# A graph layer whose gathers are issued by GpSimd: the low edge part in two halves, and one wait of VectorE removed

## The chip, the cores and the metric
The kernel runs on one core of a Trainium2 chip. Its time is the device time of one execution in microseconds (us). Three runs of the kernel before gave 1126.44, 1127.38 and 1129.05 us; the median is 1127.38 us.

The core's engines are named as the profile names them: PE (TensorE, matrix products; PEld is its weight load), DVE (VectorE), ACT (ScalarE), POOL (GpSimd) and SP (SyncE, which issues transfers here). Each runs its own list of instructions in order, and they wait for one another by semaphores.

## The reference
There are 6250 nodes with 256 features and 106250 edges, sorted by their target node `dst`. All is in float32.

```
h   = relu(layernorm(x))                          # 6250 x 256
eq  = h @ Wq + bq ;  ek = h @ Wk + bk             # per node
e   = edge_attr_256 @ We + be                     # per edge, 106250 x 256
m   = relu(eq[dst] + ek[src] + e)                 # per edge
ft  = segment_sum(m, dst, 6250)                   # per node
out = x + ft @ Wr + br
```

`src` is random, so the rows `ek[src]` have to be gathered.

## The kernel before
**Start.** The nodes' `ek` and the first rows of `eq` are computed and stored in tables in HBM (`k_table`, `q_table`). This takes some 70 us. The rest of `eq` is computed beside the edge loop.

**Edge loop.** The edges are taken in 208 groups of 512 (the last one has 3 tiles of 128 edges instead of 4). Four groups make a body; in `visit(it, u)`, `n` is the number of the group and `slot` is `n % 4`. Numbers are split in two parts for the products: a high part rounded to the format that PE multiplies, and a low part with what is left, so that each product is made of three (high x high, high x low, low x high). For one group:

- SP loads the edge features, already turned (`edge`, 4 buffers, `load_edge`, L416), the targets' positions (`rel_row`) and a window of 48 rows of `eq` (`q_win`).
- POOL writes the four gathers of the rows of `ek` (`gather`, L701; the instruction is at L714), one for each tile of 128 edges, into `k_rows`. Four buffers; it may go on when group n - 4 has been added (`s_pre`). Each gather counts up `s_wrote` when its descriptors are written, and `s_rows` when its rows have landed. Group 0 has no gather from the table: it is computed at the start from rows of `x` that four gathers brought (L654), which count up `s_wrote` too.
- ACT makes the high edge part (`edge_hi`, L809) two groups ahead, and DVE the low edge part (`edge_low`, L1155, `edge_lo = edge - edge_hi`, L1159), also two groups ahead, in one instruction over 128 x 1024.
- PE makes the product (`edge_product`, L1441), with a last matmul that picks the rows of `q_win`. It is made one group ahead. It waits for the low message part of group n - 2 (`s_mlo`), whose `p_edge` buffer it takes over.
- DVE adds the gathered rows to the product (`add_rows`, L1172, the addition at L1184), ACT makes the high message part (`m_hi`, L866), DVE the low one (`message_low`, L1188, at L1193).
- DVE makes a matrix of ones and zeros (`send`, L1167) by which PE sums the messages into a window of 48 nodes (`window_sum`); the sum is turned by PE and DVE adds it to `ft` (L1208). Once per body a block of 128 nodes goes through `Wr` to the output.

**Order on VectorE.** It is written out by hand. For group u of a body: add_rows(u), send(u), the ft addition of group u - 3, edge_low(u + 2), message_low(u), and then, in some groups of a body, one or two small instructions (L1226, L1215, L1232, L1238, L1243). PE's order for the same step is edge_product(u + 1), window_sum(u - 1), turn of u - 2.

**The wait that is removed.** Before the addition for group n, DVE waits for `s_wrote >= 4 (n + 2)`, that is until all gathers of group n + 1 have been written (LEAD is 2 and TILES is 4), besides the waits for the product of group n (`s_prod`) and for its own rows having landed (`s_rows`). In the last body this wait is left out for the last two groups.

**Why PE has no wait for the low edge part.** On DVE, edge_low(n) stands before message_low(n - 2), and PE waits for the latter; so only the first two groups wait for `s_elo`.

Of the kernel before, what the change touches and what calls it, by code (L numbers as in the profile page):

```python
# [26 lines left out]
HALVES = D // LANES  # L27
BLOCKS = 52
ROWS = BLOCKS * LANES
TILES = 4  # L30
GROUP = TILES * LANES
GROUPS = -(-EDGES // GROUP)
UNROLL = 4
# [31 lines left out]
LEAD = 2  # L65
# [21 lines left out]
def gnn_program(nc, x, dst_groups, dst_lanes, src_lanes, edges, Wq, bq, Wk, bk, We, be, Wr, br, out):  # L87
    F32, F32R = mybir.dt.float32, mybir.dt.float32r
# [14 lines left out]
    with ctx:  # L103
        def sb(name, shape, dt):
            return ctx.enter_context(nc.sbuf_tensor(name, shape, dt))
# [4 lines left out]
        def sem(name):  # L110
            return ctx.enter_context(nc.semaphore(name))
# [58 lines left out]
        edge = sb("edge", [LANES, 4, HALVES, GROUP], F32)  # L170
        edge_hi = sb("edge_hi", [LANES, 2, HALVES, GROUP], F32R)
        edge_lo = sb("edge_lo", [LANES, 2, HALVES, GROUP], F32R)
# [108 lines left out]
        s_wrote = sem("gather_descriptors_written")  # L281
        s_go_act = sem("scalar_may_go_on")
        s_idx = sem("idx_ready")
        s_ehi = sem("edge_hi_ready")
        s_elo = sem("edge_lo_ready")
# [24 lines left out]
        def after(eng, semaphore, n):  # L310


            if isinstance(n, int) and n < 0:
                return
            eng.wait_ge(semaphore, n + 1)
# [17 lines left out]
        def visit(it, u):  # L333

            body, slot = it + u // UNROLL, u % UNROLL
            return body, slot, body * UNROLL + slot, body // BODIES, body % BODIES
# [41 lines left out]
        def _(sp):  # L378
# [37 lines left out]
            def load_edge(it, u):  # L416
                body, slot, n, _, gb = visit(it, u)

                after(sp, s_elo, n - 4)
                g = gb * UNROLL + slot  # L420
                src = edges[g] if isinstance(g, int) else edges[bass.ds(g, 1)].rearrange("a p h e -> (a p) h e")
                sp.dma_start(edge[:, slot], src).then_inc(s_edge[slot], 16)
# [561 lines left out]
        def _(dve):  # L984
# [167 lines left out]
            window_starts()  # L1152
            window_table()

            def edge_low(it, u):  # L1155
                body, slot, n, _, _ = visit(it, u)

                after(dve, s_ehi, n)
                nc.vector.tensor_tensor(edge_lo[:, slot % 2], edge[:, slot], edge_hi[:, slot % 2].bitcast(F32),  # L1159
                                        ALU.subtract).then_inc(s_elo, 1)  # L1160

            def make_send(it, u):
# [9 lines left out]
            def add_rows(it, u, last=False):  # L1172
                body, slot, n, _, _ = visit(it, u)
                tiles = LAST_TILES if last and u == UNROLL - 1 else TILES
                cols = slice(0, tiles * D)

                if not (last and u + LEAD >= UNROLL):
                    dve.wait_ge(s_wrote, TILES * (n + LEAD))
                after(dve, s_prod, n)
                if isinstance(n, int) and n == 0:  # L1180
                    after(dve, s_kcopy, ALL_BLOCKS - 1)
                else:
                    dve.wait_ge(s_rows[slot], 16 * TILES * (body if slot > 0 else body - 1) + 16 * tiles)
                nc.vector.tensor_tensor(p_edge[:, slot % 2, cols], p_edge[:, slot % 2, cols],  # L1184
                                        k_rows[:, slot].rearrange("p t d -> p (t d)")[:, cols], ALU.add)\
                    .then_inc(s_pre, 1)

            def message_low(it, u, tiles=TILES):  # L1188
                _, slot, n, _, _ = visit(it, u)
                cols = slice(0, tiles * D)  # L1190

                after(dve, s_mhi, n)
                nc.vector.scalar_tensor_tensor(m_lo[:, slot % 2, cols], p_edge[:, slot % 2, cols], 0.0,  # L1193
                                               m_hi[:, slot % 2, cols].bitcast(F32), ALU.max, ALU.subtract)\
                    .then_inc(s_mlo, 1)

            def window_of(it, u):
                _, slot, _, ps, gb = visit(it, u)
                w = dve.value_load(win_tab[0:1, bass.ds(gb * UNROLL + slot, 1)], min_val=0, max_val=NODES - WIN)
                return window_start(dve, w, ps)  # L1200
# [19 lines left out]
            def finish(it):  # L1220

                after(dve, s_outp, it)
                dve.wait_ge(s_xo, (it + 1) * 16)
                if not (isinstance(it, int) and it == 0):
                    dve.wait_ge(s_out, it * 16)
                nc.vector.tensor_tensor(result[:, 0, :], p_res, out_x[:, 0, :], ALU.add).then_inc(s_fin, 1)  # L1226
# [24 lines left out]
            def steps(it, first=False, q=False):  # L1251
                for u in range(UNROLL):
                    if not (first and u < 3):
                        w0 = window_of(it, u - 3)
                    if u == 3 and isinstance(it, int) and it <= CLEAR_BODIES:
                        dve.wait_ge(s_cleared, it + 1)
                    if u == 2:
                        after(dve, s_fhi, it)
                    if u == 3:
                        after(dve, s_flo, it)  # L1260
                    add_rows(it, u)
                    make_send(it, u)
                    if not (first and u < 3):
                        add_sum(it, u - 3, w0)
                    edge_low(it, u + 2)
                    message_low(it, u)
                    if u == 0 and isinstance(it, int) and it < CLEAR_BODIES:
                        clear(it + CLEAR_AHEAD)
                    if u == 0 and first:
                        dve.wait_ge(s_unused, 1)  # L1270
                    if u == 3 and first:
                        output_bias_low()
                    if u == 1 and q:
                        next_h_low(it)
                    if u == 3 and q:
                        next_q_low(it)
                    if u == 2:
                        if not first:
                            finish(it - 1)
                        ft_low(it)  # L1280
# [10 lines left out]
            nc.vector.tensor_tensor(rel_idx[:], dst_idx[:], win_f[:].unsqueeze(2).to_broadcast(  # L1291
                [LANES, GROUPS, TILES]), ALU.subtract).then_inc(s_prep, 1)
            for u in range(2):
                edge_low(0, u)
            dve.wait_ge(s_hn0, ALL_PAIRS)
            dve.wait_ge(s_hn1, ALL_PAIRS)
            clear(0, CLEAR_AHEAD)
# [4 lines left out]
            for it in range(1, STATIC_BODIES):  # L1302
                steps(it, q=it < Q_BODIES)
# [11 lines left out]
            def last_steps(it):  # L1315
                for u in range(3):
                    w0 = window_of(it, u - 3)
                    if u == 2:
                        after(dve, s_fhi, it)
                    add_rows(it, u, True)  # L1320
                    make_send(it, u)
                    add_sum(it, u - 3, w0)
                    if u < 2:
                        edge_low(it, u + 2)
                        message_low(it, u)
                finish(it - 1)
                ft_low(it)
                w0 = window_of(it, 0)
                add_rows(it, 3, True)
                after(dve, s_flo, it)  # L1330
                dve.wait_ge(s_fhi, it + 2)
                add_sum(it, 0, w0)
                message_low(it, 2)
                add_sum(it, 1, window_of(it, 1))
                make_send(it, 3)
                message_low(it, 3, LAST_TILES)
                add_sum(it, 2, window_of(it, 2))
                finish(it)
                tail_low(0)
                w0 = window_of(it, 3)  # L1340
                after(dve, s_flo, it + 1)
                add_sum(it, 3, w0)
                for t in range(1, len(TAIL)):
                    tail_low(t)
# [10 lines left out]
        def _(pe):  # L1355
# [85 lines left out]
            def edge_product(it, u, tiles=TILES):  # L1441
                body, slot, n, _, _ = visit(it, u)


                if isinstance(n, int) and n < 2:
                    after(pe, s_elo, n)
                after(pe, s_pick, n)
                pe.wait_ge(s_win[slot], 32 * (body + 1))
                after(pe, s_mlo, n - 2)
                for j in range(tiles):  # L1450
                    target = p_edge[:, slot % 2, j * D:(j + 1) * D]
                    tile = slice(j * LANES, (j + 1) * LANES)
                    split_product(target, lambda h: edge_hi[:, slot % 2, h, tile],
                                  lambda h: edge_lo[:, slot % 2, h, tile], we_hi, we_lo, stop=False)
                    ins = nc.tensor.matmul(target, pick[:, slot % 2, tile], q_win[:, slot, :],  # L1455
                                           start=False, stop=True)
                ins.then_inc(s_prod, 1)
# [145 lines left out]
```

## Time and profile before
| | |
|---|---|
| three runs | 1126.44, 1127.38, 1129.05 us |
| profiled execution | 1127.15 us |
| its span | 1125.3 us |
| granted TensorE clock, mean | 0.998 of full speed |
| PE busy | 1085.7 us (96%) |
| DVE busy | 952.0 us (85%) |
| ACT busy | 855.8 us (76%) |
| POOL busy | 843.3 us (75%) |
| DMA | 308.88 MB, 274 GB/s on average |

The times of instructions come from one profiled execution; its time was 1127.15 us, of which the span of the profile is 1125.3 us. "Busy" is the time in which an engine ran instructions; the issue of DMAs and the handling of semaphores is not in it, except that POOL's gathers count while their descriptors are written. "Idle before" with a name after it says which engine's work or which transfer ended an idle time.

### The profile page before, as it was taken

To read this page: it belongs to the slowest core of one execution; us is meant where nothing else is said; L and a number is where in the kernel's file an instruction comes from. 1 tells how busy PE (TensorE), PEld (TensorE's weight loads), DVE (VectorE), ACT (ScalarE), POOL (GpSimd) and SP (SyncE) were. 2 spreads that over 40 slices of the span, in tenths; PEclk is the share of its full clock that TensorE was granted. 3 is DMA by queue.
4 is the path that set the end of the run, shared out by engine and by line. 5 is a ranking of instruction groups with operands and counts; after the bars stand their busy time and mean duration, and the time that the engine had idled before them with its cause. 6 is when DMAs were issued, how large, how long until landed. Compare 5 with 4: busy or idle time off the path is not lost.

```text
span 1125.3 us, 28375 instructions
## 1 busy us (share of the span) xinstructions
PE 1085.7 (96%) x9170; PEld 1063.5 (95%) x9170; DVE 952.0 (85%) x1425; ACT 855.8 (76%) x1373; POOL 843.3 (75%) x947
## 2 busy tenths in 40 slices
PE   8989999999999999999999999999999999999997
PEld 8989999999999999999999999999999999998997
DVE  7878888888888888888888888888888888887886
ACT  7968877777777777777777778777787777876774
POOL 8877777777777777777777777777777777777773
PEclk9999999999999999999999999999999999999999
DMA  9889999999999999999999899999898998998882
GB/s 299 267 241 304 288 281 275 286 276 288 278 282 285 278 285 278 280 282 276 287 277 280 284 272 288 274 283 285 271 290 274 285 287 273 288 278 268 265 252 86
DMA packets 170744, 308.88 MB, mean 274 GB/s; under 512 B 30568, under 2 KB 116981, under 8 KB 170661
## 3 DMA queue, kind: packets, MB, share of 16 engines
q1 hardware_dynamic: 130212, 198.57, 53.4%
q0 software_dynamic: 39888, 108.97, 35.8%
q14 instruction: 69, 0.56, 0.1%
q10 hardware_dynamic: 560, 0.52, 0.1%
q8 instruction: 15, 0.25, 0.1%
HBM read 280.99 MB, written 26.95 MB: 274 GB/s over the span
## 4 chain that ended last, share of the span: by engine, by line
POOL 72%; issue 24%; PE 1%; DVE 1%; ACT 1%; DMA 1%; POOLq 0%; ACTq 0%; DVEq 0%; SPq 0%
POOL k_rows L714 69%; POOL hn L641 1%; PE p_sum L1360 0%; POOL window_cols L592 0%; DMA src_idx<-in_src_lanes 0%; POOL edge L654 0%; PE p_edge L1360 0%; ACT k_rows L784 0%; ACT hn L757 0%; PE p_sum L1476 0%; DVE stats L1002 0%; PE p_turn L1380 0%; DVE m_lo L1193 0%; DMA k_rows<-k_table,idx 0%; POOL norm L619 0%
## 5 line engine op out<-in xcount | busy, mean ns | idle before, releaser
L714 POOL DMA_INDIRECT k_rows<-k_table,src_idx x796 | 764.1, 960 | 242.8 <-issue 242.8
L1360 PE MATMUL p_edge<-we_hi,edge_hi 128*128 128x256 f32 x1662 | 471.7, 284 | 28.6 <-DVE m_lo L1193 27.3
L1360 PE MATMUL p_edge<-we_hi,edge_lo 128*128 128x256 f32 x1662 | 461.3, 278 | 0.0
L1360 PE MATMUL p_edge<-we_lo,edge_hi 128*128 128x256 f32 x1662 | 460.0, 277 | 0.0
L1184 DVE TENSOR_TENSOR p_edge<-p_edge,k_rows 128x1024 f32<-128x1024 f32 x208 | 256.1, 1231 | 153.5 <-DMA k_rows<-k_table,src_idx 112.8
L866 ACT ACTIVATE m_hi<-p_edge 128x1024 fp32r<-128x1024 f32 x208 | 213.8, 1028 | 204.6 <-DVE p_edge L1184 204.6
L1360 PEld LDWEIGHTS p_edge<-we_hi,edge_hi 128*128 128x128 f32 x1662 | 313.4, 189 | 46.6 <-ACT pick L858 21.4
L1360 PEld LDWEIGHTS p_edge<-we_lo,edge_hi 128*128 128x128 f32 x1662 | 314.3, 189 | 0.0
L1360 PEld LDWEIGHTS p_edge<-we_hi,edge_lo 128*128 128x128 f32 x1662 | 312.1, 188 | 0.0
L1159 DVE TENSOR_TENSOR edge_lo<-edge,edge_hi 128x1024 fp32r<-128x1024 f32 x208 | 253.5, 1219 | 0.0
L1193 DVE SCALAR_TENSOR_TENSOR m_lo<-p_edge,m_hi 128x1024 fp32r<-128x1024 f32 x208 | 253.3, 1218 | 0.0
L1455 PE MATMUL p_edge<-q_win,pick 98*128 98x256 f32 x831 | 233.2, 281 | 0.0
L809 ACT ACTIVATE edge_hi<-edge 128x1024 fp32r<-128x1024 f32 x208 | 217.8, 1048 | 2.3 <-PE p_edge L1455 2.2
L1476 PE MATMUL p_sum<-m_hi,send 128*48 128x256 f32 x831 | 200.7, 278 | 0.6 <-DVE m_lo L1193 0.6
L1476 PE MATMUL p_sum<-m_lo,send 128*48 128x256 f32 x831 | 200.4, 278 | 0.0
L1455 PEld LDWEIGHTS p_edge<-q_win,pick 98*128 98x128 f32 x831 | 156.0, 188 | 0.0
L855 ACT ACTIVATE rel_g<-rel_row,lane_node 96x512 int16<-96x512 int16 x208 | 147.2, 708 | 4.5 <-DMA rel_row<-rel_table 4.5
L858 ACT ACTIVATE pick<-rel_g 96x512 fp32r<-96x512 int16 x208 | 131.6, 633 | 6.6
L873 ACT ACTIVATE sum_rows<-p_sum 48x256 f32<-48x256 f32 x208 | 77.3, 372 | 33.3 <-PE p_sum L1476 29.7
L1476 PEld LDWEIGHTS p_sum<-m_hi,send 128*48 128x48 f32 x831 | 101.2, 122 | 0.9 <-DVE m_lo L1193 0.9
L1476 PEld LDWEIGHTS p_sum<-m_lo,send 128*48 128x48 f32 x831 | 101.0, 121 | 0.0
L1465 PE MATMUL p_turn<-ident,sum_rows 128*128 128x128 f32 x416 | 79.4, 272 | 0.9 <-ACT sum_rows L873 0.9
(159 smaller groups left out, 1111.2 us busy)
## 6 DMA issues: line engine op xcount, KB each, us to landing
edge<-in_edges SPq DMA_DIRECT2D x208, 512.0 KB, 5.2
rel_row<-rel_table SPq DMA_DIRECT2D x208, 96.0 KB
q_win<-q_table SPq DMA_DIRECT2D x416, 48.0 KB
k_rows<-k_table,src_idx POOLq DMA_INDIRECT x796
q_table<-hn SPq DMA_DIRECT2D x46, 256.0 KB
pre<-in_x SPq DMA_DIRECT2D x55, 128.0 KB, 3.7
out_rows<-pre SPq DMA_DIRECT2D x55, 128.0 KB, 1.7
k_table<-k_rows SPq DMA_DIRECT2D x23, 256.0 KB, 3.5
```

Of the source, the lines that this page charges most:

```text
L714: nc.gpsimd.indirect_dma_start(out=k_rows[:, slot, j, :], out_offset=None, in_=k_table, in_offset=bass.IndirectOffsetOnAxis(ap=offsets, ax ...
L809: nc.scalar.activation(edge_hi[:, slot % 2], edge[:, slot], ACT.Copy).then_inc(s_ehi, 1)
L855: nc.scalar.activation(gap[:], rel_row[:, slot, :], ACT.Abs, scale=-1.0, bias=lane_node[:, bass.ds(ps, 1)]).then_inc(s_gap, 1)
L858: nc.scalar.activation(pick[0:2 * WIN, slot % 2, :], gap[:], ACT.Relu, bias=1.0, scale=-1.0)\
L866: nc.scalar.activation(m_hi[:, slot % 2, cols], p_edge[:, slot % 2, cols], ACT.Relu).then_inc(s_mhi, 1)
L1159: nc.vector.tensor_tensor(edge_lo[:, slot % 2], edge[:, slot], edge_hi[:, slot % 2].bitcast(F32), ALU.subtract).then_inc(s_elo, 1)
L1184: nc.vector.tensor_tensor(p_edge[:, slot % 2, cols], p_edge[:, slot % 2, cols], k_rows[:, slot].rearrange("p t d -> p (t d)")[:, cols], AL ...
L1193: nc.vector.scalar_tensor_tensor(m_lo[:, slot % 2, cols], p_edge[:, slot % 2, cols], 0.0, m_hi[:, slot % 2, cols].bitcast(F32), ALU.max, A ...
L1360: ins = nc.tensor.matmul(target, a(h), b[:, h, :], start=(start and h == 0 and n == 0), stop=(stop and h == HALVES - 1 and n == 2))
L1455: ins = nc.tensor.matmul(target, pick[:, slot % 2, tile], q_win[:, slot, :], start=False, stop=True)
L1465: ins = nc.tensor.transpose(p_turn[:, 0, h * LANES:(h + 1) * LANES], sum_rows[:, slot % 2, h * LANES:(h + 1) * LANES], ident[:])
L1476: ins = nc.tensor.matmul(p_sum[0:WIN, 0, 0:D], send[:, slot % 2, j, :], m[:, slot % 2, j * D:(j + 1) * D], start=(j == 0 and m is m_hi), s ...
```

## The change
It has two parts. The low edge part is computed in two instructions of 128 x 512 instead of one of 128 x 1024: the first before the low message part, the second behind it. The semaphore `s_elo` therefore counts two for each group, and those who wait for it are adapted: SP before it loads the next edges into the buffer, and PE, which now waits for the second half before every edge product, since that half no longer stands before message_low. The other part: the wait of DVE for `s_wrote` is taken out of `add_rows`.

```diff
@@ load_edge (SP)
-                after(sp, s_elo, n - 4)
+                after(sp, s_elo, HALVES * (n - 4) + HALVES - 1)
@@ edge_low (VectorE)
-            def edge_low(it, u):
+            def edge_low(it, u, h):
                 body, slot, n, _, _ = visit(it, u)
-                after(dve, s_ehi, n)
-                nc.vector.tensor_tensor(edge_lo[:, slot % 2], edge[:, slot], edge_hi[:, slot % 2].bitcast(F32),
+                if h == 0:
+                    after(dve, s_ehi, n)
+                nc.vector.tensor_tensor(edge_lo[:, slot % 2, h], edge[:, slot, h], edge_hi[:, slot % 2, h].bitcast(F32),
                                         ALU.subtract).then_inc(s_elo, 1)
@@ add_rows (VectorE)
-                if not (last and u + LEAD >= UNROLL):
-                    dve.wait_ge(s_wrote, TILES * (n + LEAD))
                 after(dve, s_prod, n)
@@ steps (VectorE), and the same in last_steps for u < 2
-                    edge_low(it, u + 2)
+                    edge_low(it, u + 2, 0)
                     message_low(it, u)
+                    edge_low(it, u + 2, 1)
@@ before the loop (VectorE)
             for u in range(2):
-                edge_low(0, u)
+                for h in range(HALVES):
+                    edge_low(0, u, h)
@@ edge_product (PE)
-                if isinstance(n, int) and n < 2:
-                    after(pe, s_elo, n)
+                after(pe, s_elo, HALVES * n + HALVES - 1)
                 after(pe, s_pick, n)
```

## Rows read from the trace of the kernel before

**Rows 1.** The page's first parts: span, busy time by engine, chain that ended last.
```profile
span 1125.3 us, 28375 instructions
...
PE 1085.7 (96%) x9170; PEld 1063.5 (95%) x9170; DVE 952.0 (85%) x1425; ACT 855.8 (76%) x1373; POOL 843.3 (75%) x947
...
POOL 72%; issue 24%; PE 1%; DVE 1%; ACT 1%; DMA 1%; POOLq 0%; ACTq 0%; DVEq 0%; SPq 0%
```

**Rows 2.** Waits, whole run: who waited for whom: us in total, times, longest.
```profile
POOL k_rows L714 <- issue: 252.0, 826, 0.6
...
PE p_edge L1360 <- DVE m_lo L1193: 27.3, 59, 1.3
```

**Rows 3.** The gathers' line: duration ns min/median/max, first and last start us.
```profile
L714 POOL DMA_INDIRECT k_rows<-k_table,src_idx x796: 942/946/1966, 64.5 to 1069.8; - x199
```

**Rows 4.** Gathers by stretch: stretch, us, POOL busy (x instructions), clock, DMA.
```profile
64.40:79.60 15.20, 11.95 (x11) 0.89 0.78 230
79.60:130.20 50.60, 39.27 (x37) 1.00 0.96 299
...
sum 1045.50, POOL 793.58; mean POOL 132.26
```

**Rows 5.** Timeline, one group of the steady part: start us, us, instruction.
```profile
501.88 1.23 DVE L1184 TENSOR_TENSOR p_edge<-p_edge,k_rows 128x1024 f32<-128x1024 f32 x1 [0.80 <-DMA k_rows<-k_table,src_idx]
502.15 0.94 POOL L714 DMA_INDIRECT k_rows<-k_table,src_idx  x1 [0.30 <-issue]
503.02 0.35 DVE L1167 TENSOR_TENSOR send<-rel_idx,window_cols 128x192 fp32r<-128x192 f32 x1
503.15 1.03 ACT L866 ACTIVATE m_hi<-p_edge 128x1024 fp32r<-128x1024 f32 x1 [1.07 <-DVE p_edge L1184]
503.29 0.25 DVE L1208 TENSOR_TENSOR ft<-ft,p_turn 128x96 f32 x1
503.40 0.95 POOL L714 DMA_INDIRECT k_rows<-k_table,src_idx  x1 [0.30 <-issue]
503.45 1.22 DVE L1159 TENSOR_TENSOR edge_lo<-edge,edge_hi 128x1024 fp32r<-128x1024 f32 x1
...
504.59 1.22 DVE L1193 SCALAR_TENSOR_TENSOR m_lo<-p_edge,m_hi 128x1024 fp32r<-128x1024 f32 x1
...
505.72 0.42 DVE L1232 TENSOR_TENSOR hT_lo<-p_sum,hT_hi 128x256 fp32r<-128x256 f32 x1
```

**Rows 6.** Timeline around two long gathers of the steady part.
```profile
387.67 1.02 POOL L714 DMA_INDIRECT k_rows<-k_table,src_idx  x1 [0.30 <-issue]
387.78 0.25 DVE L1208 TENSOR_TENSOR ft<-ft,p_turn 128x96 f32 x1
...
1032.44 1.79 POOL L714 DMA_INDIRECT k_rows<-k_table,src_idx  x1 [0.30 <-issue]
...
1033.32 1.22 DVE L1193 SCALAR_TENSOR_TENSOR m_lo<-p_edge,m_hi 128x1024 fp32r<-128x1024 f32 x1
```

**Rows 7.** Timeline before the loop: a gather beside instructions of 128x512.
```profile
66.67 0.68 DVE L1287 TENSOR_TENSOR we_lo<-k_rows,we_hi 128x512 fp32r<-128x512 f32 x1
67.12 1.05 POOL L714 DMA_INDIRECT k_rows<-k_table,src_idx  x1 [0.30 <-issue]
67.27 0.69 DVE L1289 TENSOR_TENSOR wr_lo<-k_rows,wr_hi 128x512 fp32r<-128x512 f32 x1
```

**Rows 8.** Timeline: the additions of groups 188 and 189, and what precedes the first.
```profile
1018.69 0.95 POOL L714 DMA_INDIRECT k_rows<-k_table,src_idx  x1 [0.30 <-issue]
...
1019.67 1.23 DVE L1184 TENSOR_TENSOR p_edge<-p_edge,k_rows 128x1024 f32<-128x1024 f32 x1 [0.97 <-DMA k_rows<-k_table,src_idx]
...
1025.90 1.23 DVE L1184 TENSOR_TENSOR p_edge<-p_edge,k_rows 128x1024 f32<-128x1024 f32 x1 [2.03 <-DMA k_rows<-k_table,src_idx]
```

**Rows 9.** Timeline of the end: the last gather and the last addition.
```profile
1108.79 0.95 POOL L714 DMA_INDIRECT k_rows<-k_table,idx  x1 [0.30 <-issue]
...
1113.01 0.97 DVE L1184 TENSOR_TENSOR p_edge<-p_edge,k_rows 128x768 f32<-128x768 f32 x1 [0.29 <-PE p_edge L1455]
```

More of the change, by code:

```diff
@@ L1323, in last_steps @@
                     if u < 2:
-                        edge_low(it, u + 2)
+                        edge_low(it, u + 2, 0)
                         message_low(it, u)
+                        edge_low(it, u + 2, 1)
                 finish(it - 1)
```

## The prediction
> **What bounds the kernel now.** I read the engine table first. PE looks like the bound at 96%, DVE stands at 85% and POOL only at 75%, yet the chain that ended last is 72% POOL and 24% "issue" [rows 1]. So next come the waits: POOL's gathers wait for nothing but their own issue, 252.0 us over 826 gaps, 0.305 us each, never more than 0.6 [rows 2]. GpSimd is never idle for want of work: a gather takes 0.942 us at the least and 0.946 at the median [rows 3], call it 0.945, so one starts every 1.25 us. There are 206 groups of four and a last one of three, 827 gathers. The account of the span of 1125.3 us [rows 1] closes: 64.5 us until the first [rows 3], then 827 x 0.945 = 781.5 of writing, 251.9 of gaps and 12.1 of something else (busy sum 793.58 less 781.5, [rows 4]), until the last ends at 1109.74, then 15.6 us to the end of the span at 1125.3 [rows 9]. PE and DVE idle a little in each group and are paced by GpSimd: PE's waits for m_lo are 27.3 us in all [rows 2].
>
> **What the 12.1 us are** decides this case, because whatever lengthens one gather lengthens the kernel by as much. Look at the long ones. The gather at 1032.44 took 1.79: it began while the low edge part ran, and ended 0.91 after m_lo began at 1033.32. The one at 387.67 took 1.02, begun while `send` ran, and ended 0.91 after the ft addition of 387.78 began [rows 6]. The one at 67.12 took 1.05, begun while L1287 ran (128x512, half the size of an edge part), and ended 0.90 after L1289 began [rows 7]. A free gather ends 0.945 after its own start. So a gather asks for something 0.045 us after its start; if a VectorE instruction of that kind has it, it waits until the next VectorE instruction begins, then needs 0.90. The holders (edge_low L1159, send L1167, L1287) read two operands from SBUF. Those that read PSUM don't hold: the gather of 502.15 starts in the middle of the k addition (501.88) and takes 0.94 [rows 5].
>
> The Trainium skill, page "SBUF — State Buffer", section "Who interferes with whom", has a rule for it and one against it: a VectorE instruction with two SBUF inputs contends with a GpSimd instruction that reads SBUF, but a tensor_tensor is said not to stall descriptor generation. By the second, no placing of edge_low could cost anything and the time would stay about 1126 (before, less the 1 us of the end below). Rows 6 and 7 speak against it.
>
> In the steady state these holders are nearly harmless, 6.2 us in 195 groups (12.1 less the first two stretches of [rows 4]: 11.95 - 11 x 0.945 = 1.6, and 39.27 - 37 x 0.945 = 4.3). The removed wait is why. VectorE's add waits until the next group's gathers are written: at 1019.67 it starts 0.03 after the gather of 1018.69 ends [rows 8]. That pins VectorE to GpSimd's clock. Counted from the add (501.88), send starts at 1.14, ft at 1.41, edge_low at 1.57, m_lo at 2.71 and the next thing at 3.84 [rows 5]. A gather starts at 1.52 and asks at 1.565, a hair before edge_low; the next asks at 2.81, after edge_low let go at 2.71. The 1.14 us of edge_low lies exactly between two requests. Where VectorE was not pinned, from 79.6 to 130.2, the same work cost 4.3 us in 37 gathers, 0.47 per group [rows 4].
>
> **The change, part by part.**
> *The wait taken away.* The add then starts when its own rows have landed (or its product is there, or VectorE is free). Rows were written 5.03 us before the add; landing takes between at most 3.3 us (last group: written 1109.74, added 1113.01, [rows 9]) and 6.3 (written 1019.64, added at 1025.90 after waiting 2.03 for the DMA, [rows 8]). So VectorE moves ahead by 1 to 1.7 us in most groups, and its place against GpSimd's 1.25 us grid is set by a landing time that varies by 3 us, over two periods of the grid. I take the phase as uniform. VectorE's lead itself is worth nothing in the steady part: no gather waits for it.
>
> *The halves.* A 128x512 of this kind takes 0.68 and the next starts 0.60 after it [rows 7]. Counted from the add: first half 1.57 to 2.17; m_lo has to wait for m_hi, which ends at 503.15 + 1.03, that is 2.30, so it starts at about 2.34; it takes 1.13 to the next start (505.72 - 504.59), so second half 3.47 to 4.07. VectorE's step grows by 0.23 (4.07 against 3.84), and PE, which now waits for the second half where it waited for m_lo, is released 0.23 later per group. PE's own waits for m_lo are 27.3 us in 208 groups, so PE had room in most, and a group that lasts 0.2 longer on GpSimd gives all of it back: nothing. If that cover were gone it would cost at most 0.23 x 207 = 48. The edge load on SP waits for the second half; it stands in SP's queue behind the window loads, which wait for the product of the group before, so it is seldom late, and there are four edge buffers, so that its data is needed some three groups later: nothing.
>
> *What the halves cost GpSimd at a uniform phase.* Requests come every 1.25 us; let the first fall evenly over 1.14 to 2.39 after the add, the holders being send 1.14-1.41, halves 1.57-2.17 and 3.47-4.07:
> - first request in send (0.27 wide): waits 0.135 on average, is let go at 1.41, the third then falls at 3.91 in the second half and waits 0.16: 0.295
> - 1.41 to 1.57 (0.16 wide): free, the third falls at 3.91 to 4.07: 0.08
> - in the first half (0.60 wide): waits 0.30; let go at 2.17, the next asks at 3.42, just before the second half: 0.30
> - 2.17 to 2.39 (0.22 wide): the next falls at 3.42 to 3.64, three quarters of them wait about 0.51: 0.40
> Together (0.27 x 0.295 + 0.16 x 0.08 + 0.60 x 0.30 + 0.22 x 0.40) / 1.25 = 0.29 us per group. From the other side, the unpinned stretch gave 0.47 per group with whole parts; a hold of length w costs w²/2.5 at a uniform phase, two of 0.60 against one of 1.14 are 0.55 of it: 0.26. I take 0.275. Bounds: at the one lucky phase nothing is caught, 0; if m_lo began right after the first half, the request at 3.42 would fall into the second as well and add 0.60 x 0.48 / 1.25 = 0.23, 0.52.
>
> *The end.* In the last body the wait was absent already for its last two groups. VectorE comes to them about a microsecond earlier; the last add (1113.01) waited for the product, whose release hung on VectorE [rows 9]. Bounds 0 and -1.7 (the lead), I take -1.
>
> **Sum** against the profiled execution (1127.15 = span 1125.3 + 1.85): 207 x 0.275 = 56.9 of holds in place of 12.1, +44.8; end -1; 1170.9, and the median of the runs lies 0.2 above that execution: 1171. GpSimd stays the bound.
>
> **Rivals.**
> *Both halves hit.* The phase is not uniform but leans to where the second half catches too (0.43 us per group and more, up to 0.52): 1127 + 107.6 - 12.1 - 1 = 1222 at the end of it, from 1203. For it: the request after the first half escapes by 0.05 only. Against it: m_hi's 1.03 us is very steady.
> *Not slower.* Landing settles at a lag that puts requests just before send's end and before each half: a lag of about 3.7 us would: the add then starts 3.8 us after its rows were written, and the fifth request after that writing, 5.34 later, falls 1.5 after the add, where it falls now. Then hardly anything is caught, the first stretches lose their 5.9 us to about 3 and the end gives 1: 1123 to 1126. It decides from under 0.06 us per group. For it: 3.7 lies among the lags seen. Against: the good window is some 0.1 wide in 1.25, and the landing times spread over 3 us.
> *The wait bound nothing.* If most landings came as late as the wait, VectorE would stay in its place and only the halves would be new; at the pinned phase the requests at 1.565, 2.81 and 4.06 miss the first half and graze the end of the second by 0.01: 1127 to 1138 with the late landings. Against: the add starts 0.03 after a gather's end, and waits that long for nothing else.
>
> **How the numbers follow.** Forecast 0.75 (0.12 to 0.43 per group: 1139 to 1203), both halves 0.08, not slower 0.10, nothing bound 0.07. Range 1138 to 1203: it leaves out both-halves and the not-slower case. A measurement tells about 0.2% (2.3 us) from no change. Faster by over that 0.06, within it 0.05, slower 0.89.
>
> **What would show it.** In the changed trace: gathers of 1.0 to 1.6 us in most groups, each ending 0.90 after a VectorE start that follows an edge_low half or send; the minimum still 0.942; POOL busy about 838 us, gaps still 0.305 and "issue"; PE's and ACT's waits longer; the add starting at landing, not at a gather's end. Wrong if the gathers' mean stays under 0.96, or POOL gets waits of another kind, or PE's waits for edge_lo set a pace while GpSimd idles.

## The result, and the profile after

The changed kernel is slower. Six runs took 1161.42 to 1169.9 us, median 1165.48, against 1128.2 (1126.44 to 1130.88) for six of the kernel before; the ratio is 1.0326, 95% interval 1.0297 to 1.0356. The profiled execution took 1169.9 us (span 1168.1), at the upper end of its runs. The sums below are made on that one.

The page of the changed kernel answers to [rows 1]. PE's busy time hardly moves (1085.7 to 1094.4), VectorE's rises by 30 us (208 more instructions, with their fixed part), and POOL's by 41.0:
```profile
span 1168.1 us, 28717 instructions
...
PE 1094.4 (94%) x9170; PEld 1067.8 (91%) x9170; DVE 982.2 (84%) x1633; ACT 857.2 (73%) x1373; POOL 884.3 (76%) x947
```
The waits of the changed kernel, answering to [rows 2]; columns are us in total, times, longest:
```profile
POOL k_rows L714 <- issue: 241.1, 790, 0.6
...
DVE p_edge L1183 <- DMA k_rows<-k_table,src_idx: 114.0, 111, 2.9
...
PE p_edge L1362 <- DVE edge_lo L1160: 54.5, 76, 2.1
...
POOL k_rows L714 <- DVE p_edge L1183: 11.6, 34, 1.5
```
GpSimd is still never idle, but for one wait. Of the 34 waits put down to VectorE, 33 are the 0.305 of every other gap; the longest, 1.5 us near 80 us, is a real wait. PE's wait for VectorE doubled (54.5 for edge_lo, where it was 27.3 for m_lo), and did not set the time, as run a below shows.

The gathers' line and their busy time by stretch answer to [rows 3, 4] (stretch, us, POOL busy (x), clock, DMA share, GB/s):
```profile
L714 POOL DMA_INDIRECT k_rows<-k_table,src_idx x796: 942/946/1475, 64.2 to 1109.7; - x199
```
```profile
64.20:79.60 15.40, 11.87 (x12) 0.89 0.76 240
79.60:130.20 50.60, 37.97 (x38) 1.00 0.91 283
130.20:1152.20 1022.00, 784.99 (x778) 1.00 0.87 266
sum 1088.00, POOL 834.84; mean POOL 278.28
```
Minimum and median are what they were; the sum rose by 834.84 - 793.58 = 41.3 us. The longest is 1.475 where it was 1.966, so a half adds 0.53 at most where a whole edge part added 1.02. This is one held gather in the timeline of the changed kernel:
```profile
609.54 0.68 DVE L1160 TENSOR_TENSOR edge_lo<-edge,edge_hi 128x512 fp32r<-128x512 f32 x1
609.92 1.11 POOL L714 DMA_INDIRECT k_rows<-k_table,src_idx  x1 [0.30 <-issue]
610.14 0.41 DVE L1225 TENSOR_TENSOR pre<-p_turn,pre 128x256 f32<-128x256 f32 x1
```
It starts in the second half, and ends 0.81 after that half's end (0.89 after the next VectorE instruction begins). Counted over the timeline, 159 gathers were lengthened by over 25 ns with a half of edge_lo running, by 48.9 us together; 18 with send (1.9), 25 with L1214 (1.5), which is another small instruction with two SBUF inputs (hT_lo from ft and hT_hi).

### The profile page after: what moved, and what is told of

Its sections match the earlier page's. It is cut to its first block and busy times, and to the rows that moved or that the text cites. A ratio compares the mean times of both kernels' runs of the same rounds, so it can differ in the third digit from the quotient of the medians.

```text
span 1168.1 us, 28717 instructions
## 1 busy us (share of the span) xinstructions
PE 1094.4 (94%) x9170; PEld 1067.8 (91%) x9170; DVE 982.2 (84%) x1633; ACT 857.2 (73%) x1373; POOL 884.3 (76%) x947
## 5 line engine op out<-in xcount | busy, mean ns | idle before, releaser
L714 POOL DMA_INDIRECT k_rows<-k_table,src_idx x796 | 802.8, 1009 | 244.2 <-issue 232.6
L1362 PE MATMUL p_edge<-we_hi,edge_hi 128*128 128x256 f32 x1662 | 475.3, 286 | 60.7 <-DVE edge_lo L1160 54.5
L1362 PEld LDWEIGHTS p_edge<-we_hi,edge_hi 128*128 128x128 f32 x1662 | 315.0, 190 | 82.6 <-ACT pick L858 43.8
L866 ACT ACTIVATE m_hi<-p_edge 128x1024 fp32r<-128x1024 f32 x208 | 213.1, 1024 | 174.5 <-DVE p_edge L1183 173.3
L1160 DVE TENSOR_TENSOR edge_lo<-edge,edge_hi 128x512 fp32r<-128x512 f32 x416 | 284.8, 685 | 0.5 <-ACT edge_hi L809 0.5
```

Source lines behind the costliest of these rows:

```text
L714: nc.gpsimd.indirect_dma_start(out=k_rows[:, slot, j, :], out_offset=None, in_=k_table, in_offset=bass.IndirectOffsetOnAxis(ap=offsets, ax ...
L866: nc.scalar.activation(m_hi[:, slot % 2, cols], p_edge[:, slot % 2, cols], ACT.Relu).then_inc(s_mhi, 1)
L1160: nc.vector.tensor_tensor(edge_lo[:, slot % 2, h], edge[:, slot, h], edge_hi[:, slot % 2, h].bitcast(F32), ALU.subtract).then_inc(s_elo, 1)
L1362: ins = nc.tensor.matmul(target, a(h), b[:, h, :], start=(start and h == 0 and n == 0), stop=(stop and h == HALVES - 1 and n == 2))
```

## The experiments

Theory P: the time lost is gathers held by VectorE instructions with two SBUF inputs, at a phase that the wait used to fix. Rival R: it is PE's later release by the second half.

**a_halves_wait_kept.** The changed kernel, with the wait back in `add_rows`:
```diff
+                if not (last and u + LEAD >= UNROLL):
+                    dve.wait_ge(s_wrote, TILES * (n + LEAD))
                 after(dve, s_prod, n)
```


> The low edge part in two halves, as in the changed kernel, but VectorE still waits until the next group's gathers are written. Theory P (the loss is gathers held by VectorE instructions with two SBUF inputs, at a phase that the wait no longer fixes): the wait pins VectorE, requests fall at 1.565, 2.81 and 4.06 us after the addition, the halves lie at 1.57 to 2.17 and 3.47 to 4.07, so hardly anything is held: 1126 to 1131 us. Rival R (the loss is PE's later release: it waits for the second half where it waited for the low message part, 0.23 us later in each group, 0.18 x 207 = 37 us): about 1165 us, as the changed kernel.

1137.09 us; ratio to before 1.0078 (1.0061 to 1.0094). So the halves, PE's wait for them included, are worth 9 of the 37 us at most. R has fallen where GpSimd is the bound; but P's range was missed by 6 us too. The trace of this run says why:
```profile
601.77 0.68 DVE L1160 TENSOR_TENSOR edge_lo<-edge,edge_hi 128x512 fp32r<-128x512 f32 x1
602.18 1.09 POOL L714 DMA_INDIRECT k_rows<-k_table,src_idx  x1 [0.30 <-issue]
...
602.37 0.42 DVE L1239 TENSOR_TENSOR hn<-p_sum,hn 128x256 fp32r<-128x256 f32 x1
```
The addition does not always start 0.03 after the gather's end; in two of the four groups of each body it starts 0.09 or 0.19 after, as it does in the kernel before. Then the request that I put at the very end of the second half (4.06 of 4.07) comes while the half still runs, 0.15 before it lets go in the group shown. The gathers' busy sum is 803.16 less 781.5 = 21.6 us of holds, 9.6 more than before, of a span that is 11.3 longer; gaps are 1.4 of the rest, the end 0.3.

Counted gather by gather, the holds from 200 us on are 5.6 us in the kernel before and 14.5 in run a, and the second halves make 11.5 of the latter. The start is no gain either (from 79.6 to 200 us, 4.9 of holds before, 6.6 in run a): with halves VectorE needs until 202 us to catch up and be pinned, where before it needed 120. One whole edge part fits between two gathers with some 0.2 us to spare. Two halves 1.9 us apart leave only 0.08 of that at the place where the wait puts the gathers, which the groups whose addition starts 0.03 after a gather's end just meet and the later ones miss; another 0.12 lies where a gather starts just behind the first half, and was not tried. (These are estimates from the widths in the paragraph on when a gather is held, below.)

**b_whole_no_wait.** The kernel before, without the wait:
```diff
-                if not (last and u + LEAD >= UNROLL):
-                    dve.wait_ge(s_wrote, TILES * (n + LEAD))
```


> Only the wait is removed, the low edge part stays one instruction of 128x1024. Theory P: the phase is free and one hold of 1.14 us is worse than two of 0.60; at a uniform phase 0.53 us per group, by the unpinned stretch of the kernel before 0.47: 1127 + 97 to 110 - 12 = 1205 to 1228 us, slower than the changed kernel. Rival R: PE is released as before, so about 1127 us.

1222.66 us; ratio 1.0805 (1.0750 to 1.0861), inside P's range. Its gathers, their line and then the sum of their busy time:
```profile
L714 POOL DMA_INDIRECT k_rows<-k_table,src_idx x796: 942/946/1994, 64.6 to 1163.2; - x199
```
```profile
sum 1236.00, POOL 889.92; mean POOL 296.64
```
889.92 - 781.5 = 108.4 us of holds, 0.52 per group; the uniform phase said 0.53. The removed wait is therefore the part of the change that costs, some 94 us by itself, and the halves win 57 of them back. The two parts do not add up: with the wait, halves cost 9; without it, they win 57.

**c_halves_no_input.** The changed kernel, with the loop's halves made by an instruction without inputs:
```diff
+                if isinstance(it, int) and n < 2:
                     nc.vector.tensor_tensor(edge_lo[:, slot % 2, h], edge[:, slot, h],
                                             edge_hi[:, slot % 2, h].bitcast(F32), ALU.subtract).then_inc(s_elo, 1)
+                else:
+                    nc.vector.memset(edge_lo[:, slot % 2, h].bitcast(F32), 0.0).then_inc(s_elo, 1)
```


> The changed kernel, no wait, halves, but from group 2 on each half of the low edge part is a memset of the same 128x512 (no input; the low part of the edges is left out of the result). A memset of 128x512 took 0.48 us in the trace of before, a half 0.68, so VectorE's step is 0.4 us shorter too. Theory P: nothing but send and the small L1214 holds gathers any more, 0.04 us per group: gathers' mean falls from 1.01 to about 0.955 us, total 1122 to 1128 us though the wait is gone. Rival R: PE is still released by the second half, some 0.2 us earlier than in the changed kernel: 1127 to 1165, gathers' mean no longer the cause. Rival D (transfers collide when VectorE runs ahead): 1165 us.

This kernel leaves out the low edge part from group 2 on. 1120.1 us; ratio 0.9927 (0.9910 to 0.9943): 2 us below P's range, and 0.7% faster than before, though the wait is gone. A gather that starts in a memset takes 0.95:
```profile
602.82 0.48 DVE L1164 MEMSET edge_lo<- 128x512 f32 x1
602.98 0.95 POOL L714 DMA_INDIRECT k_rows<-k_table,src_idx  x1 [0.30 <-issue]
```
Its sum of gathers is 789.64, 8.1 us of holds. That is 45.2 less than in the changed kernel, and its time is 45.4 less: the holds are the whole loss. The 0.2 us less for each half is hardly the reason, since VectorE waited 114 us for rows in the changed kernel. PE still waits for the second half, and the DMA engines are no less busy (share 0.92 from 400 to 1050 us, 0.87 in the changed kernel), so neither PE's release nor colliding transfers cost the 45 us. VectorE's lead is there too, but smaller (over groups 100 to 199 the addition starts 0.15 us before the next group's last gather ends, at the median, where it was 0.77).

**d_edge_low_before_send.** The kernel before, one line moved in `steps`:
```diff
                     add_rows(it, u)
+                    edge_low(it, u + 2)
                     make_send(it, u)
                     if not (first and u < 3):
                         add_sum(it, u - 3, w0)
-                    edge_low(it, u + 2)
```


> The kernel before, with its wait, and one change of order: the low edge part stands before send and the ft addition instead of behind them, so it lies at 1.14 to 2.28 us after the addition instead of 1.57 to 2.71. Theory P: pinned at a bad phase; the request at 1.565 is held in every group until 2.28, 0.71 us: 1127 - 6 + 207 x 0.71 = 1268 us (1250 to 1275), one gather in four 1.66 us long. Rivals R and D: same instructions, same waits, PE released at the same time: 1127 us.

1270.88 us; ratio 1.1259 (1.1240 to 1.1278); 1268 was expected. A group of this run:
```profile
599.65 1.23 DVE L1184 TENSOR_TENSOR p_edge<-p_edge,k_rows 128x1024 f32<-128x1024 f32 x1 [1.46 <-DMA k_rows<-k_table,src_idx]
599.93 0.94 POOL L714 DMA_INDIRECT k_rows<-k_table,src_idx  x1 [0.30 <-issue]
600.80 1.22 DVE L1159 TENSOR_TENSOR edge_lo<-edge,edge_hi 128x1024 fp32r<-128x1024 f32 x1
601.17 1.66 POOL L714 DMA_INDIRECT k_rows<-k_table,src_idx  x1 [0.30 <-issue]
601.93 0.35 DVE L1167 TENSOR_TENSOR send<-rel_idx,window_cols 128x192 fp32r<-128x192 f32 x1
```
The same instructions, the same waits; the edge part starts 0.43 earlier after the addition, so the gather of 601.17 begins inside it instead of 0.05 ahead of it, and pays 0.71. Nearly every group has one such gather, and they are 0.75 longer on average, since some additions start 0.19 and not 0.03 after a gather's end. This is the strongest of the runs for the phase as such.

**Where to pin, and whether it can be made better.** Four kernels moved the wait by one gather or used the halves only in the unpinned start:
```diff
 e, o, r:  -  dve.wait_ge(s_wrote, TILES * (n + LEAD))    +  dve.wait_ge(s_wrote, TILES * (n + LEAD) - 1)
 f:        -  dve.wait_ge(s_wrote, TILES * (n + LEAD))    +  dve.wait_ge(s_wrote, TILES * (n + LEAD) + 1)
 g:        the kernel of run a, with halves for n < 14 and one whole instruction, counting 2, from there
 h, p:     g and f together
```


> The kernel before with its wait for one gather less: VectorE's addition may start when three of the next group's four gathers are written, 1.25 us earlier, which is the same place on GpSimd's grid. Theory P with landing: the phase is right only where the rows have landed by then, 3.78 us after they were written; the landing times spread around that, so about half of the groups start late and at a free phase, where a whole low edge part costs some 0.5 us: 0.25 us per group on average, 1127 + 52 = 1165 to 1190 us. Rival (any pin on the grid will do, landing is no matter): 1127 us.

> The kernel before with its wait for one gather more (VectorE 1.25 us later, same place on the grid). Theory P with landing: rows that land up to 6.2 us after they were written are then covered too, so of the 6.2 us of holds after 130 us about half go; the first stretch, where VectorE is behind anyway, stays; the end may lose up to 1 us: 1123 to 1127 us against 1128 for before. Rival (VectorE's lag is what costs, a smaller lead must be slower): 1130 us or more.

> The kernel before with its wait, the low edge part in two halves only for groups below 14, where VectorE is behind and not pinned; from there whole. Theory P: in the unpinned stretch halves cost 0.27 us per group (changed kernel, 79 to 131 us) against 0.45 (before), 13 groups: -2.4 us; VectorE's step is 0.2 us longer there, so it catches up a group or two later, +0.5 to 1: 1126 to 1128 us. Rival (VectorE's longer step is what costs): 1130 us.

> Both together: halves for groups below 14 and the wait for one gather more. Theory P: the gains add, 1121 to 1126 us. Rival: slower than before, 1130 us or more.

These four ran on a chip where the kernel before itself took 1522.85 us at a granted clock near 0.91, as did the later runs, on two more chips (1563.44 and 1516.11). There the question can't be asked: PE falls to 1.2 GHz again and again (in run f the granted clock is 1.00 from 500 to 505 us and 0.50 from 525 to 530), VectorE's additions come 11 to 19 us after the next group's gathers, and GpSimd waits for them. The ratios: e 1.0013 (0.9968 to 1.0058), f 1.0057 (1.0009 to 1.0105), g 1.0121 (1.0072 to 1.0171), h 1.0043 (1.0005 to 1.0081). The two repeats:

> The kernel of e_pin_one_gather_earlier, since there the kernel before itself took 1523 us at a granted clock of 0.91 and PE was the bound. As there: theory P with landing says 1165 to 1190 us where the kernel before takes 1128, about half of the groups being late; the rival (landing is no matter) 1127 us.

> The kernel of h_halves_at_the_start_pin_later again (halves for groups below 14, wait for one gather more), for the same reason. Theory P: 1121 to 1126 us against 1128; the rival 1130 or more.

o 1.0010 (0.9955 to 1.0064), p 1.0080 (1.0040 to 1.0121). All lie within 2% of the kernel before, and on a chip where GpSimd is the bound they stay untried (runs i to n, the same two kernels, gave no time): where the best pin lies, and whether the 12 us of holds that are left can be won, is open.

**q_changed_again and r_pin_earlier.** The changed kernel unaltered, and e once more.

> The changed kernel once more, unaltered, beside the kernel before. Theory P: where the kernel before takes 1128 us and GpSimd is the bound, 1165 us again. Where the chip grants TensorE a clock of about 0.9 and the kernel before takes 1520 to 1565 us, GpSimd waits hundreds of us for VectorE, PE is the bound, and a gather that is held costs nothing: within 1% of the kernel before. Rival R (the loss is PE's later release by the second half): there PE is the bound, so the loss must be larger than 37 us: 1560 us or more beside 1520.

> The kernel of e_pin_one_gather_earlier. Where the kernel before takes 1128 us: theory P with landing says 1165 to 1190 us, about half of the groups being late; the rival (landing is no matter) 1127 us. Where it takes 1520 us or more, no difference, as in e_pin_one_gather_earlier.

q: 1574.98 us; ratio 1.0376 (1.0307 to 1.0446). P expected no difference here, and is wrong for this regime; R's number (1560 or more beside 1520) came out. r: 0.9900 (0.9851 to 0.9950). The waits of q, then of r (us in total, times, longest):
```profile
POOL k_rows L714 <- DVE p_edge L1183: 432.4, 114, 6.6
...
PE p_edge L1362 <- DVE edge_lo L1160: 38.0, 31, 2.3
```
```profile
POOL k_rows L714 <- DVE p_edge L1184: 331.6, 102, 6.6
```
and the stretch from 200 to 1000 us of q, then of r (us, PE, PEld, DVE, ACT, POOL busy (x), granted clock, DMA share, GB/s):
```profile
200.00:1000.00 800.00, 659.52 (x4543) 611.60 (x4542) 494.22 (x791) 422.89 (x654) 429.74 (x439) 0.86 0.62 193
```
```profile
200.00:1000.00 800.00, 679.42 (x4839) 626.91 (x4840) 510.39 (x724) 447.40 (x696) 477.13 (x464) 0.91 0.66 205
```
GpSimd waits for VectorE for over 330 us in both, so it isn't the bound, and q's gathers are held less than r's (35 us against 68). What costs there must lie elsewhere, by the waits on the loop of PE and VectorE: the second half that PE must wait for, VectorE's longer step, and a clock of 0.86 against 0.91 in the same stretch are the candidates. Which of them, whether the lower clock is cause or consequence, and what the removed wait has to do with it, these runs don't tell apart: runs a and b had no counterpart on such a chip. A release 0.23 us later per group is 48 us by the prediction's own bound, and 59 were lost.

## Why the prediction was right

**The bound and the mechanism** were read rightly: GpSimd stays the bound, its gathers are held by instructions with two SBUF inputs, and their phase against GpSimd's grid decides the cost. Runs b, c and d, 150 us apart, come out within 1% of their numbers.

**When a gather is held, and when it is let go,** was not read rightly. The prediction has it ask 0.045 us after its start, and go on when the next VectorE instruction begins. Where VectorE idles behind the holder, the second can be seen to fail (changed kernel):
```profile
595.53 0.68 DVE L1160 TENSOR_TENSOR edge_lo<-edge,edge_hi 128x512 fp32r<-128x512 f32 x1
595.75 1.29 POOL L714 DMA_INDIRECT k_rows<-k_table,src_idx  x1 [0.30 <-issue]
596.59 1.23 DVE L1192 SCALAR_TENSOR_TENSOR m_lo<-p_edge,m_hi 128x1024 fp32r<-128x1024 f32 x1 [0.38 <-ACT m_hi L866]
```
The gather ends 0.82 after the half's end and only 0.45 after m_lo begins. Mostly the next instruction begins 0.08 before the recorded end of the one ahead of it, and then 0.82 and 0.90 look alike, as in [rows 6, 7]. The first fails here:
```profile
413.88 0.75 DVE L1160 TENSOR_TENSOR edge_lo<-edge,edge_hi 128x512 fp32r<-128x512 f32 x1
413.90 0.95 POOL L714 DMA_INDIRECT k_rows<-k_table,src_idx  x1 [0.31 <-issue]
```
The gather starts 0.02 into the half and is not held. What the traces do show: a gather is held if it starts more than some 0.035 us after the holder's start and at least 0.125 before its end, and then it ends 0.82 after that end. By this alone, 4948 of the 4962 gathers in the traces of before, of the changed kernel and of runs a to d come out within 0.02 us, 858 of them held; 10 of the 14 others lie before 67 us, beside instructions of the start. In 92 of the 205 lengthened gathers of the changed kernel VectorE idled behind the holder, so this was no rare case; the prediction's own sum lets the first half go at 2.17, and not at 2.34 where it puts m_lo. So a half holds over 0.52 us and not 0.60, a whole edge part over 1.06 and not 1.14, send over 0.19 and not 0.27. At a uniform phase the prediction's sum would have given 0.22 per group with these widths, not 0.29.

**The holds.** Forecast 0.275 us per group, 56.9 in all; measured 834.84 - 781.5 = 53.3, 0.26 per group. The uniform phase was an approximation: of 170 groups counted (30 to 199), the first request fell 28 times in send, 23 in the gap, 68 in the first half and 51 behind it, where evenly it would be 37, 22, 82 and 30. The second half was hit the more: it held gathers for 29.3 us, the first for 19.6. Of the two estimates, 0.29 from the phases and 0.26 from the unpinned stretch, the second hit it, and that is luck in part: widths too large by 0.08 (some 14 us too much in the first estimate) and a phase that was not uniform (some 8 us above it with the right widths) partly cancel.

**VectorE's lead.** I said 1 to 1.7 us. Over groups 40 to 199 the addition started 0.76 before the end of the next group's last gather at the median, and in nine of ten groups between 1.8 before and 0.0 after it; before, it started 0.09 after it at the median. It moved ahead by 0.85, less than forecast. The forecast did not say that VectorE would be behind and not ahead for the first 25 groups: the addition of group 1 came 14.6 us after its rows were written, and the lag was used up only near 200 us, since its longer step gains little on GpSimd. For the holds this was no matter.

**The end** is the term that failed. Forecast -1 us; the stretch after the last gather went from 15.6 to 16.0 us. The last addition did come sooner after the last gather (2.70 us against 3.28 in [rows 9]), released by the landing. But VectorE's lead had let PE run dry while it waited for those rows. PE's busy time and granted clock at the end of the changed kernel (columns as above):
```profile
1150.00:1157.00 7.00, 4.05 (x34) 3.64 (x32) 4.23 (x9) 2.52 (x4) 1.78 (x2) 1.00 0.34 96
1157.00:1160.40 3.40, 2.84 (x12) 2.31 (x13) 1.40 (x5) 0.38 (x1) 0.00 (x0) 0.52 0.00 0
1160.40:1168.00 7.60, 3.88 (x29) 3.18 (x27) 3.10 (x9) 1.10 (x3) 0.00 (x0) 0.95 0.20 70
```
PE was busy 4.05 of 7 us, and then had 1.2 GHz for 3.4 us, in the middle of the last window sums, whose matmuls follow each other every 0.21 us:
```profile
1157.55 0.42 PE L1477 MATMUL p_sum<-m_hi,send 128*48 128x256 f32 x1
1157.76 0.42 PE L1477 MATMUL p_sum<-m_lo,send 128*48 128x256 f32 x1
```
In the kernel before they follow every 0.115 us at 2.4 GHz. Eight of them lose 0.8 us, some of the next six a part of that. That the idle PE brought the lower clock is read from the order of things; no run tested it.

**The sum** against the profiled executions: first gather 0.3 sooner, holds +41.3, gaps +1.4 (the one real wait is 1.2 of it; the forecast had nothing here), end +0.4: +42.8, from 1125.3 to 1168.1. Forecast +43.8. The closeness owes something to luck, since holds too large by 3.6 and the end too good by 1.4 partly cancel, and the median of the runs lies 4.4 below the profiled one.

**The rivals.** "Both halves hit" (0.43 and more per group), "not slower" and "the wait bound nothing" are excluded by the 0.26 per group. The third had said 1127 to 1138 for halves at a pinned phase; run a, which is that case, took 1137.

**PE's later release** was costed at nothing under cover of GpSimd, 48 us without it. Run a bears out the first; run q lost 59, of which this may be the larger part.

## What to carry to other kernels

When GpSimd writes gathers back to back, look at the longest of them and at what VectorE was running when they began: an instruction with two SBUF inputs can be free or cost 0.7 us per group, depending on a start 0.4 us earlier or later (run d). A wait that looks superfluous may be what keeps two engines in step; before it is taken out, measure where the held instruction falls against the other engine's grid, and if the phase can't be fixed, make the holders short (without the wait, two halves cost 0.26 us per group, one whole 0.52) or without a second SBUF operand. A rule for a wait that was read from a few lines should be tried on every instruction of the trace: that a gather is let go at the holder's end, and not at the next start, shows twice in the trace of before (the gathers at 70.02 and 90.43 us, with VectorE idle behind the holder). A cost that is hidden behind one bound may come back where another chip's clock moves the bound.

## What the runs showed of the hardware that was not expected

- Nearly always, whether a gather is held is decided about when it starts. An edge part that starts 0.05 after the gather's start runs its full 1.22 us at once and the gather its 0.945 [rows 5]; and 41 gathers of the six traces that started up to 0.031 us after a holder were not held either. The Trainium skill, page "SBUF — State Buffer", section "SBUF: two separate sides", has whichever starts first keep the pair for its whole instruction while the other fully blocks; here only the gather blocked, and VectorE was slowed at most from 0.684 to 0.746 us (the maximum of the 416 halves), where both began together (by up to 0.08 us in the other instructions and runs).
- A held gather ends 0.82 us after the holder's end, whatever VectorE does next: 0.814 to 0.829 over the 177 gathers of the changed kernel that edge_lo and send held.
- A memset of 128x512 doesn't hold a gather (0.95 us beside it, run c): 152 gathers of that run start while one runs, and none of them took over 0.96 us. One more, at 91.94 us, starts 0.005 before one and took 1.58; it ended 0.81 after the end of an hT_lo with two SBUF inputs that had begun 0.41 after the gather's start. Why this one was held is open.
- On three of four chips the kernel before took 1516 to 1563 us, on the fourth 1128, at granted clocks of 0.88 to 0.92 against 0.998. The clock's mean alone, 10% lower, does not account for 35% more time; what else PE lost there is not settled.
